# First attention in six slots a batch: row maxima in three fillings of 500 columns, weighted sums in one row

## The chip, the cores and the metric

The kernel runs on one core of a Trainium2 chip. Engines named here: TensorE (PE, with its weight loads PEld), VectorE (DVE), ScalarE (ACT), GpSimd (POOL) and SyncE (SP, which issues most DMAs). The metric is the device time in microseconds of one execution, the median of the runs shown.

## What is computed

Two transformer layers on x of 8 batches x 112 rows x 256 (f32), with a context of 8 x 375 x 256. The part that the change touches is the first of the two attentions, on layer-normalised x, with 16 heads of width 16:

```
q_ = (q @ Wq.T + bq).reshape(B, Sq, HEADS, D_K).transpose(0, 2, 1, 3)
k_ = (k @ Wk.T + bk).reshape(B, Sk, HEADS, D_K).transpose(0, 2, 1, 3)
v_ = (v @ Wv.T + bv).reshape(B, Sk, HEADS, D_K).transpose(0, 2, 1, 3)
scores = jnp.einsum('bhqd,bhkd->bhqk', q_, k_) / jnp.sqrt(jnp.float32(D_K))
attn = jax.nn.softmax(scores, axis=-1)
ctx = jnp.einsum('bhqk,bhkd->bhqd', attn, v_)
...
x = x + _L0_xattn_ref(_layernorm(x), ctx_1024, ctx_1024, ...)
x = x + _L0_ffn_ref(_layernorm(x), ...)      # 8 experts, top 1, 112 rows each
x = x + _L1_xattn_ref(_layernorm(x), ctx_1024, ctx_1024, mask, ...)
x = x + _L1_ffn_ref(_layernorm(x), ...)
```

## The kernel before

**Stages.** After loads and layer norms the first attention runs over the 8 batches (`NB`), and in the same loop each batch's output projection, second layer norm and expert routing follow. Then come the 8 experts, the second attention and the last feed-forward layer. Nothing of the later three stages is edited, except how many blocks of the second attention's value projection (`project_context`, "context projections", 24 in all, each of the shape of a V block) are pulled into gaps of the first.

**The 16 heads** are four groups `g` of four heads `j`; group g = 2m + a. `kt[b % 3]` and `qz` hold K and Q with the heads at rows 32j to 32j + 31, so that four matmuls of one group sit in four row groups of PE and write banks 0 to 3 of PSUM, one each. `qz` holds zeros in the rows of the other parity `a`.

**Three works share banks 0 to 3** in turn:

- `row_max(b, g)` on PE: for a group, 112 x 375 scores per head, only to find the row maxima. DVE reduces them into `mneg` (L1056). Four fillings a batch (MX).
- `scores(b, step)` on PE: the scores transposed (125 keys x 2 x 112 queries, two blocks a step, three steps a batch), to which a matmul of `onesc` with `maxT` adds the negative maxima. ACT takes the exponential into `pT` (L833). Three fillings a batch (ST).
- `weighted(b, step)` on PE reads `pT` and `vones` and adds into bank 4 (PV). It fills none of banks 0 to 3. `pT` has two buffers.

The banks are drained in two halves, LOW (banks 0, 1) and HIGH (2, 3): each has its own semaphores `filled` and `drained`. PE opens a half when the half's last user has drained it (`open_tiles`), and a reader waits for the half's `filled`. So a batch has seven fillings of banks 0 to 3, and each waits for the reader of the one before.

**The slots.** The order is written out by hand. `steps()` runs i from -1 over u in range(SLOTS), and every engine goes through the same list: in slot u of step i PE does `scores(i, SCORE_AT[u])`, `row_max(i + 1, MAX_AT[u])`, `weighted(i, WEIGHTED_AT[u])` and then the stages of `PIPE[u]`, each for batch i minus the number beside it. ACT does in the same slot `exps` and then its share of the stages, DVE `row_max` and then its share. What an engine does is in program order, so a stage's place in `PIPE` is its place in each engine's queue.

**The stages of PIPE.** V0 to V2: V's three blocks. K0, K1: K's two halves. QX, QP: transposes of x and Q for two batches. ND0/ND1 (DVE): the maxima of m = 0, 1 cut into two bf16 pieces (L1069, L1070). NM0/NM1: PE transposes them, ACT copies them to `maxT` (L862). U (ACT, L841): copies bank 4 to `ctxU`. C1: PE transposes `ctxU` after `read(("PV", b))`, that is, after U; DVE divides by the sums (L1075, L1078). C2, C3: transpose and output projection. C4, C5: transpose of the second norm and gate logits. L2, D5, C6, D6: norm and routing. These PE stages use banks 5 to 7 in rotation.

**Loads.** SP asks for the weights of expert e (e = 0 to 3, into `ring`) when scores (e, 0) are filled.

## Time and profile before

| | us |
|---|---|
| median of 3 runs | 377.79 (377.69 to 378.69) |
| the profiled execution | 375.65 |
| its span in the trace | 373.9 |
| PE busy | 354.1 (95%) |
| DVE busy | 182.5 (49%) |
| ACT busy | 149.7 (40%) |
| POOL busy | 57.6 (15%) |

The chain that ended last is PE for 85% of the span. The first attention takes about the first 200 us of it. A PE matmul in f32 appears in the trace as two instructions, so that "x8" is four matmuls. A group's row gives the start of its first instruction, the time to the end of its last, and idle time of the engine just before, in brackets. Groups overlap a little, so the distance between two starts is the time that a group really takes.

### The profile page before, as it was taken

What the parts mean: (1) busy time and instruction counts of PE and PEld (TensorE: products, weight loads), DVE (VectorE), ACT (ScalarE), POOL (GpSimd) and SP (SyncE); (2) the same over time, 40 slices, a digit from 0 to 9 for tenths busy, and PEclk for the clock granted to TensorE, in tenths of its full rate; (3) what the DMA queues carried; (4) which work ended last, traced back from release to release, by engine and by line L of the source; (5) the groups of instructions that cost most, each with busy time, mean ns of one, the idle gap of its engine ahead of it and who ended that gap; (6) DMA issues with size and microseconds to landing.
All of it is one profiled execution on the core that took longest, in us unless ns stands there. A gap on an engine that the chain in (4) does not pass through costs nothing.

```text
span 373.9 us, 7935 instructions
## 1 busy us (share of the span) xinstructions
PE 354.1 (95%) x3108; PEld 266.4 (71%) x3108; DVE 182.5 (49%) x573; ACT 149.7 (40%) x361; POOL 57.6 (15%) x95
## 2 busy tenths in 40 slices
PE   3889999999999999998889999999889999999996
PEld 2446666766657665755668998998768889797875
DVE  4964345647566465564462122212489667532500
ACT  0524553554454553535533221120345667523300
POOL 2730000010101000010120000030694421200000
PEclk9999999999999999999999999999999999999999
DMA  8946060603400100000207499970110011111000
GB/s 245 351 111 227 0 225 3 220 20 96 144 1 15 28 4 13 2 15 2 70 12 213 136 334 335 303 210 25 50 50 1 3 53 52 40 39 50 26 25 25
DMA packets 24885, 35.29 MB, mean 94 GB/s; under 512 B 2608, under 2 KB 21408, under 8 KB 24736
## 3 DMA queue, kind: packets, MB, share of 16 engines
q1 hardware_dynamic: 22160, 31.73, 26.9%
q0 software_dynamic: 768, 1.84, 1.7%
q10 hardware_dynamic: 1920, 1.21, 1.2%
q8 instruction: 25, 0.41, 0.4%
q14 instruction: 12, 0.10, 0.1%
HBM read 31.06 MB, written 3.72 MB: 93 GB/s over the span
## 4 chain that ended last, share of the span: by engine, by line
PE 85%; DVE 6%; DMA 5%; issue 2%; ACT 1%; POOL 0%; SPq 0%; DVEq 0%; ACTq 0%; POOLq 0%
PE ps L417 10%; PE ps L575 8%; PE ps L720 8%; PE ps L585 7%; PE ps L431 7%; PE ps L698 6%; PE ps L454 6%; PE ps L385 6%; PE ps L361 5%; PE ps L651 3%; PE ps L352 3%; DMA xres<-in_x 2%; PE ps L667 2%; PE ps L477 2%; PE ps L521 2%
## 5 line engine op out<-in xcount | busy, mean ns | idle before, releaser
L1056 DVE TENSOR_REDUCE mneg<-ps 112x2 f32<-112x750 f32 x64 | 57.1, 933 | 42.3 <-PE ps L417 41.9
L833 ACT ACTIVATE heads<-ps 125x896 f32<-125x896 f32 x48 | 41.4, 915 | 17.5 <-PE ps L437 17.5
L1273 POOL TENSOR_TENSOR rstd<-veps,neghalf 112x1 f32<-112x1 f32 x32 | 18.5, 577 | 194.1 <-DVE veps L1022 193.9
L417 PE MATMUL ps<-heads 32*112 32x375 f32 x256 | 38.5, 518 | 1.8 <-DVE mneg L1056 1.4
L431 PE MATMUL ps<-heads 32*125 32x224 f32 x384 | 32.2, 374 | 0.7 <-DVE mneg L1056 0.6
L361 PE MATMUL ps<-ctxT,w_in 128*128 128x375 f32 x64 | 25.6, 524 | 7.3 <-DMA ctxT<-in_ctxT 5.9
L575 PEld LDWEIGHTS ps<-xT,ring 128*128 128x128 f32 x256 | 29.8, 192 | 1.1 <-ACT xT L788 0.7
L575 PE MATMUL ps<-xT,ring 128*128 128x112 f32 x256 | 29.9, 275 | 0.4 <-ACT xT L788 0.4
L720 PE MATMUL ps<-heads,ring 128*112 128x256 f32 x128 | 28.8, 382 | 0.0
L585 PE MATMUL ps<-ring,heads 128*112 128x256 f32 x128 | 28.8, 379 | 0.0
L454 PEld LDWEIGHTS ps<-heads,vones 125*17 125x17 f32 x768 | 17.2, 97 | 13.9 <-issue 12.6
L431 PEld LDWEIGHTS ps<-heads 32*125 32x125 f32 x384 | 19.7, 182 | 9.9 <-issue 7.5
L720 PEld LDWEIGHTS ps<-heads,ring 128*112 128x112 f32 x128 | 22.3, 177 | 6.1 <-issue 1.4
L385 PE MATMUL ps<-w_in,ctxT 128*125 128x256 f32 x96 | 25.6, 389 | 0.0
L585 PEld LDWEIGHTS ps<-ring,heads 128*112 128x112 f32 x128 | 22.1, 177 | 4.4
L417 PEld LDWEIGHTS ps<-heads 32*112 32x112 f32 x256 | 14.1, 169 | 15.5 <-issue 9.0
L788 ACT ACTIVATE xT<-ps 128x224 f32<-128x224 f32 x40 | 13.6, 358 | 28.6 <-PE ps L352 28.4
L698 PE MATMUL ps<-xT,heads 128*128 128x224 f32 x128 | 24.9, 353 | 0.0
L454 PE MATMUL ps<-heads,vones 125*17 125x112 f32 x768 | 23.3, 260 | 1.3 <-ACT heads L833 1.3
L698 PEld LDWEIGHTS ps<-xT,heads 128*128 128x128 f32 x128 | 24.0, 190 | 0.1
L477 PE MATMUL ps<-w_in,ctxT 128*125 128x256 f32 x96 | 23.7, 386 | 0.0
L1161 DVE TENSOR_SCALAR heads<-ps,b1col 128x112 f32<-128x112 f32 x32 | 8.5, 326 | 29.8 <-PE ps L575 29.8
(140 smaller groups left out, 523.3 us busy)
## 6 DMA issues: line engine op xcount, KB each, us to landing
ring<-in_L_ffn_W SPq DMA_DIRECT2D x16, 1024.0 KB, 6.7
ctxT<-in_ctxT SPq DMA_DIRECT2D x8, 375.0 KB, 11.0
heads<-in_L_ffn_W SPq DMA_DIRECT2D x2, 1024.0 KB, 10.4
ring<-x_by_odd_rows_dram SPq DMA_DIRECT2D x4, 448.0 KB, 3.6
ring<-in_mask SPq DMA_DIRECT2D x1, 1312.5 KB, 7.4
expert_in_dram<-eo SPq DMA_DIRECT2D x1, 896.0 KB, 11.2
b2row<-in_L_ffn_b SPq DMA_DIRECT2D x8, 112.0 KB, 7.6
out_dram<-ring SPq DMA_DIRECT2D x8, 112.0 KB, 1.9
```

Source lines behind the costliest of these rows:

```text
L361: mm = pe.matmul(o[:, 0:S2], w_in[:, 1, k, m * P:(m + 1) * P], ctxT[:, k, b * S2:(b + 1) * S2], start=k == 0, stop=k == DT - 1)
L385: mm = pe.matmul(o[0:KC, 0:D], ctxT[:, k, b * S2 + c * KC:b * S2 + (c + 1) * KC], w_in[:, 2, k, :], start=k == 0, stop=k == DT - 1)
L417: mm = pe.matmul(bank(j)[0:S, 0:S2], qz[rows, m, a, b * S:(b + 1) * S], kt[b % 3][rows, m, :], start=True, stop=True)
L431: pe.matmul(bank(j)[0:KC, x * QW:(x + 1) * QW].rearrange("p (a q) -> p a q", a=2), kt[b % 3][rows, m, c * KC:(c + 1) * KC], qz[rows, m, :, ...
L454: mm = pe.matmul(bank(4)[32 * j:32 * j + VW, g * S:(g + 1) * S], vones[b % 2][0:KC, c, PAIRS * g + j, :], pT[(SCORE_STEPS * b + step) % 2] ...
L477: mm = pe.matmul(o[0:KC, 0:D], ctxT[:, k, b * S2 + c * KC:b * S2 + (c + 1) * KC], wv_at1[:, k, :], start=k == 0, stop=k == DT - 1)
L575: mm = pe.matmul(o[:, f * S:(f + 1) * S], w1e[e % RING][:, k, ft * P:(ft + 1) * P], xT[:, k, e * S:(e + 1) * S], start=k == 0, stop=k == D ...
L585: mm = pe.matmul(o[0:S, 0:D], hid[e % 2][:, ft, :], w2e[e % RING][:, ft, :], start=ft == 0, stop=ft == FT - 1)
L698: mm = pe.matmul(o[:, f * 2 * S:(f + 1) * 2 * S], w1f[:, k, ft * P:(ft + 1) * P], xT[:, k, 2 * p * S:2 * (p + 1) * S], start=k == 0, stop= ...
L720: pe.matmul(o[0:S, 0:D], gT[p % 2][:, ft, x * S:(x + 1) * S], w2f[:, ft, :], start=ft == 0, stop=False)
L833: act.activation(pT[w % 2][0:KC, pair.start:pair.stop, :], ps[0:KC, pair.start:pair.stop, 0:2 * QW], ACT.Exp, scale=DK ** -0.5).then_inc(f ...
L1056: v.tensor_reduce(mneg[:, b % 2, PAIRS * g + pair.start:PAIRS * g + pair.stop], ps[0:S, pair.start:pair.stop, 0:S2], AX.X, ALU.max, negate ...
```

## The change

- `SLOTS` is 6. The maxima of a batch come in three fillings (`MAX_PARTS`) of 500 columns: group 0 and the first 125 keys of group 1; 250 keys each of groups 1 and 2; group 3 and the last 125 keys of group 2. A filling has two matmuls for each head in place of one. DVE reduces each part apart, those of 125 keys into `mpart`, and joins the two halves of groups 1 and 2 with a minimum (L1099 of the new kernel) ahead of the pieces.
- The three weighted sums of a batch stand in a row in slot 5, so that `pT` needs a third buffer. It lies in the fourth of the experts' ring buffers; expert 3's weights are loaded when batch 6's weighted sums are done. In the last batch the sums stay spread over slots 1, 3 and 5.
- `PIPE` is rearranged. U of batch i - 1 is in slot 0, and C5 is one step later. Q's halves are in two slots (Q0, Q1), and the transposes QX earlier.
- Within scores the matmul with the maxima comes first.
- Context projections: 7 within the slots for 5, 6 ahead of the experts for 7.

```
-SLOTS = 7
+SLOTS = 6
-MAX_AT = {1: 0, 3: 1, 5: 2, 6: 3}
-WEIGHTED_AT = {1: 0, 3: 1, 5: 2}
+MAX_AT = {1: 0, 3: 1, 5: 2}
+MAX_PARTS = (((0, 0, 375), (1, 0, 125)), ((1, 125, 375), (2, 0, 250)), ((3, 0, 375), (2, 250, 375)))
+WEIGHTED_AT = {5: (0, 1, 2)}
+WEIGHTED_LAST = {1: (0,), 3: (1,), 5: (2,)}
 PIPE = {
-    0: [("NM1", 0), ("C1", 1), ("D5", 2), ("V0", -1)],
+    0: [("U", 1), ("NM1", 0), ("C5", 2), ("C1", 1), ("D5", 2), ("V0", -1)],
...
-    6: [("U", 0), ("C5", 1), ("K1", -2), ("ND1", -1)],
+    5: [("ND1", -1)],
 }
-CTX_AT = {(6, 1): 1, (6, 3): 1, (7, 0): 1, (7, 4): 2}
-CTX_BEFORE_EXPERTS = 7
+CTX_AT = {(6, 1): 1, (6, 3): 2, (7, 0): 1, (7, 2): 1, (7, 4): 2}
+CTX_BEFORE_EXPERTS = 6
...
+        pT.append(ring[:, RING - 1, 0:PAIRS * 4 * S].rearrange("p (j n) -> p j n", j=PAIRS))
...
-            def row_max(b, g):
+            def row_max(b, step):
+                for n, (g, lo, hi) in enumerate(MAX_PARTS[step]):
+                    m, a = divmod(g, 2)
+                    at = n * (MAX_PARTS[step][0][2] - MAX_PARTS[step][0][1])
+                    for half, pair in HALVES:
+                        if n == 0:
+                            open_tiles(("MX", b, step), half)
+                        for j in pair:
+                            rows = slice(32 * j, 32 * j + 32)
+                            mm = pe.matmul(bank(j)[0:S, at:at + hi - lo], qz[rows, m, a, b * S:(b + 1) * S],
+                                           kt[b % 3][rows, m, lo:hi], start=True, stop=True)
+                        if n == 1:
+                            mm.then_inc(filled[half], 1)
...
             def exps(b, step):
-                w = SCORE_STEPS * b + step
-                if w >= 2:
-                    act.wait_ge(pv_units, w - 1)
+                if b == NB - 1 and step == 2:
+                    act.wait_ge(pv_units, SCORE_STEPS * b + 1)
+                elif b:
+                    act.wait_ge(pv_units, SCORE_STEPS * (b - 1) + step + 1)
...
+                    if step == 1:
+                        top = mneg[:, b % 2, PAIRS:3 * PAIRS].rearrange("p (g j) -> p j g", j=PAIRS)[:, js, :]
+                        v.tensor_reduce(top, ps[0:S, js, 0:500].rearrange("p j (g k) -> p j g k", g=2), AX.X, ALU.max,
+                                        negate=True).then_inc(free, 1)
+                    else:
+                        top = mneg[:, b % 2, PAIRS * MAX_PARTS[step][0][0]:][:, js]
+                        v.tensor_reduce(mpart[:, step // 2, js], ps[0:S, js, 375:500], AX.X, ALU.max, negate=True)
+                        v.tensor_reduce(top, ps[0:S, js, 0:375], AX.X, ALU.max, negate=True).then_inc(free, 1)
...
-            for e in range(RING):
+            for e in range(RING - 1):
                 wait_filled(("ST", e, 0, HIGH))
                 load_expert(e)
...
+            sp.wait_ge(pv_units, SCORE_STEPS * (NB - 1))
+            load_expert(RING - 1)
```

ACT around the copy to `ctxU`, before, from the last exponential of one batch to the first two of the next (`heads<-ps 125x896` are exponentials of the two halves, `vones` is V's copy, `xT` C4's, `ex` C5's, `heads<-ps,bcol` K's):

```order
L862 ACTIVATE maxT<-ps 128x224 [waits high_tiles_filled,bank7_filled]
L841 ACTIVATE ctxU<-ps 128x448 [waits bank6_filled,pv_units_done]
L868 ACTIVATE ex,small<-lg,small 112x8 [waits logit_max_ready]
L797 ACTIVATE heads<-ps,bcol 128x375 [waits bank6_filled,high_tiles_filled]
L833 ACTIVATE heads<-ps 125x896 [waits low_tiles_filled,pv_units_done]
L833 ACTIVATE heads<-ps 125x896 [waits high_tiles_filled]
L862 ACTIVATE maxT<-ps 128x224 [waits high_tiles_filled,bank7_filled]
L817 ACTIVATE vones<-ps 125x16x16 [waits bank6_filled,pv_units_done]
```
And in the changed kernel:

```order
L888 ACTIVATE maxT<-ps 128x224 [waits high_tiles_filled,bank5_filled]
L859 ACTIVATE heads<-ps 125x896 [waits low_tiles_filled,pv_units_done]
L859 ACTIVATE heads<-ps 125x896 [waits high_tiles_filled]
L867 ACTIVATE ctxU<-ps 128x448 [waits bank5_filled,pv_units_done]
L888 ACTIVATE maxT<-ps 128x224 [waits high_tiles_filled,bank6_filled]
L894 ACTIVATE ex,small<-lg,small 112x8 [waits logit_max_ready]
L842 ACTIVATE vones<-ps 125x16x16 [waits bank6_filled,pv_units_done]
```
The copy to `ctxU` stood ahead of the two exponentials of the next batch's first scores; now it stands behind both.

PE, before, the last weighted sums of a batch, then C4, NM0, the fourth maxima filling and C5:

```order
L454 MATMUL ps<-heads,vones 17x112 [waits high_tiles_drained,low_tiles_drained]
L454 MATMUL ps<-heads,vones 17x112 x15
L352 MATMUL ps<-ident,xn 128x112 [waits bank7_drained,normalised_ready]
L352 MATMUL ps<-ident,xn 128x112
L499 MATMUL ps<-identb,mpieces 128x112 [waits bank5_drained,max_pieces_ready]
L499 MATMUL ps<-identb,mpieces 128x112
L417 MATMUL ps<-heads 112x375 [waits low_tiles_drained,bank7_drained,bank6_drained]
L417 MATMUL ps<-heads 112x375
L417 MATMUL ps<-heads 112x375 [waits high_tiles_drained]
L417 MATMUL ps<-heads 112x375
L531 MATMUL ps<-wg,xT 112x8 [waits bank6_drained,bank7_drained]
L531 MATMUL ps<-wg,xT 112x8
```
The same queue from the end of the next batch's first scores on (NM1, the transposes of C1, V's block, the first maxima filling):

```order
L499 MATMUL ps<-identb,mpieces 128x112 [waits bank5_drained,max_pieces_ready]
L499 MATMUL ps<-identb,mpieces 128x112
L507 MATMUL ps<-ident,ctxU 112x128 [waits bank6_drained,bank4_drained]
L507 MATMUL ps<-ident,ctxU 112x128 x3
L385 MATMUL ps<-w_in,ctxT 125x256 [waits bank7_drained]
L385 MATMUL ps<-w_in,ctxT 125x256
L417 MATMUL ps<-heads 112x375 [waits low_tiles_drained,bank6_drained,bank5_drained]
L417 MATMUL ps<-heads 112x375
L417 MATMUL ps<-heads 112x375 [waits high_tiles_drained]
```
In the changed kernel PE has the three weighted sums of a batch in a row, in slot 5:

```order
L479 MATMUL ps<-heads,vones 17x112 [waits bank6_drained,low_tiles_drained,high_tiles_drained,bank7_drained,bank4_drained]
L479 MATMUL ps<-heads,vones 17x112 x15
L479 MATMUL ps<-heads,vones 17x112 [waits high_tiles_drained,low_tiles_drained]
L479 MATMUL ps<-heads,vones 17x112 x15
L479 MATMUL ps<-ring,vones 17x112 [waits high_tiles_drained,low_tiles_drained]
L479 MATMUL ps<-ring,vones 17x112 x15
```
The next batch's first scores follow directly, and from their end on PE has:

```order
L524 MATMUL ps<-identb,mpieces 128x112
L556 MATMUL ps<-wg,xT 112x8 [waits bank7_drained]
L556 MATMUL ps<-wg,xT 112x8
L532 MATMUL ps<-ident,ctxU 112x128 [waits bank5_drained,bank4_drained]
L532 MATMUL ps<-ident,ctxU 112x128 x3
L405 MATMUL ps<-w_in,ctxT 125x256 [waits bank6_drained]
L405 MATMUL ps<-w_in,ctxT 125x256
L441 MATMUL ps<-heads 112x375 [waits bank5_drained,bank6_drained,low_tiles_drained]
L441 MATMUL ps<-heads 112x375
L441 MATMUL ps<-heads 112x375 [waits high_tiles_drained]
L441 MATMUL ps<-heads 112x375
L441 MATMUL ps<-heads 112x125 x4
```
The transposes reading `ctxU` (L507 before, L532 now) wait for bank 4 in both, with V's block and the next maxima filling behind them; the gate logits (`ps<-wg,xT`) now stand just ahead of them, and the filling behind has 375 and 125 columns.

## Rows read from the trace of the kernel before

**Rows 1.** Six batches: us, busy time (instructions) by engine, PE clock, DMA share, GB/s.

```profile
47.88:171.78 123.90, 122.80 (x1476) 80.13 (x1474) 71.79 (x208) 60.77 (x126) 8.44 (x11) 1.00 0.18 59
```
**Rows 2.** Order of time, PE, batch 2: start, us, engine, line, what, count, [idle before].

```profile
67.62 0.27 PE L499 MATMUL ps<-identb,mpieces 112*128 112x112 bf16 x2
67.73 0.61 PE L507 MATMUL ps<-ident,ctxU 128*112 128x128 f32 x4
68.18 1.03 PE L385 MATMUL ps<-w_in,ctxT 128*125 128x256 f32 x4
69.13 1.25 PE L417 MATMUL ps<-heads 32*112 32x375 f32 x8
70.31 0.97 PE L454 MATMUL ps<-heads,vones 125*17 125x112 f32 x32
71.21 0.41 PE L514 MATMUL ps<-ident,cc 112*128 112x112 f32 x2
...
73.19 1.12 PE L521 MATMUL ps<-w_in,ccT 128*112 128x256 f32 x4
...
75.01 0.55 PE L352 MATMUL ps<-ident,xn 112*128 112x112 f32 x4
75.49 0.90 PE L417 MATMUL ps<-heads 32*112 32x375 f32 x8
76.32 0.97 PE L454 MATMUL ps<-heads,vones 125*17 125x112 f32 x32
```
**Rows 3.** Order of time, PE, the second half of the same batch.

```profile
78.58 1.68 PE L377 MATMUL ps<-xT,w_in 128*128 128x224 f32 x8
80.19 0.66 PE L431 MATMUL ps<-heads 32*125 32x224 f32 x8
...
81.37 1.13 PE L385 MATMUL ps<-w_in,ctxT 128*125 128x256 f32 x4
82.58 1.60 PE L417 MATMUL ps<-heads 32*112 32x375 f32 x8
...
86.29 0.56 PE L531 MATMUL ps<-wg,xT 128*112 128x8 f32 x4
86.70 1.51 PE L361 MATMUL ps<-ctxT,w_in 128*128 128x375 f32 x4
```
**Rows 4.** Order of time, ACT, the first exponentials of batch 2.

```profile
67.72 1.73 ACT L833 ACTIVATE heads<-ps 125x896 f32<-125x896 f32 x2
69.33 0.36 ACT L862 ACTIVATE maxT<-ps 128x224 bf16<-128x224 bf16 x1
```
**Rows 5.** The line that copies bank 4: durations in ns, min/median/max.

```profile
L841 ACT ACTIVATE ctxU<-ps x8: 537/550/550, 44.3 to 183.9; 128x448 f32<-128x448 f32 x8
```
**Rows 6.** Order of time, DVE, batch 2.

```profile
66.32 0.16 DVE L1096 TENSOR_REDUCE small<-ps 112x1 f32<-112x8 f32 x1
...
68.45 0.26 DVE L1075 RECIPROCAL rden<-ps 112x16 f32<-112x16 f32 x1 [1.26 <-PE ps L507]
...
70.19 1.78 DVE L1056 TENSOR_REDUCE mneg<-ps 112x2 f32<-112x750 f32 x2
```
**Rows 7.** Order of time, PE: what follows the first scores of batches 0 and 1.

```profile
27.26 0.27 PE L499 MATMUL ps<-identb,mpieces 112*128 112x112 bf16 x2
...
47.88 0.27 PE L499 MATMUL ps<-identb,mpieces 112*128 112x112 bf16 x2
```
**Rows 8.** Order of time, PE, batch 7: after its first scores; its last weighted sums.

```profile
171.78 0.27 PE L499 MATMUL ps<-identb,mpieces 112*128 112x112 bf16 x2
...
173.75 0.97 PE L454 MATMUL ps<-heads,vones 125*17 125x112 f32 x32 [0.39 <-ACT heads L833]
...
183.25 0.41 PE L352 MATMUL ps<-ident,xn 112*128 112x112 f32 x2
...
184.54 0.65 PE L507 MATMUL ps<-ident,ctxU 128*112 128x128 f32 x4
```
**Rows 9.** The page's DMA issues: the experts' weights, KB each, us to landing.

```profile
ring<-in_L_ffn_W SPq DMA_DIRECT2D x16, 1024.0 KB, 6.7
```

93 lines of the change are left out of this document (45 added, 48 removed).

## The prediction

> **What bounds the kernel now.** I read first the busy time over the stretch from the end of batch 1's first scores to the end of batch 7's (six whole batches): TensorE (PE) is busy 122.80 of 123.90 us at a granted clock of 1.00 [rows 1], so 20.65 us a batch go by with hardly an idle gap. That reads as "bound by PE", but a matmul's record covers waits within a group of them. So I read the order of time next, start to start. A filling of banks 0 to 3 takes 0.83 us when nothing holds it (75.49 to 76.32 [rows 2]) and 1.54 us when the exponentials are not out of the upper half yet (82.58 to 84.12 [rows 3]). Scores take 1.18 us free (80.19 to 81.37 [rows 3]). What is under the cover of busy PE is a second chain: PE fills banks 0 to 3, ACT or DVE empties them, PE fills again. Seven such turns make a batch. The links, from end to end of the PE groups:
>
> - scores to the end of the next maxima filling: 67.62 to 70.31 = 2.69 us [rows 2]. In it the two exponentials run from 67.72 to 69.45 [rows 4], and 0.86 us of filling follow.
> - maxima to the end of the next scores: 70.31 to 73.19 = 2.88 us [rows 2]. The two reductions end at 70.19 + 1.78 = 71.97 [rows 6], and scores end 1.22 us later.
>
> Where PE has much to do between two fillings, PE's work is the longer (81.37 minus 76.32 = 5.05 us with weighted sums, K and Q [rows 2, 3]). So the kernel stands with both limits close to each other, and the question of the change is the next limit at each of the six turns.
>
> **The change, turn by turn.** *Maxima.* The columns are the same 1500 a batch, in three fillings of 500. A free filling is 0.83 us for 375 columns in two passes; 125 more columns add between 0 (hidden) and a further third of it, 0.28. I take 0.21, the streaming part alone: 1.04 us, and 0.86 + 0.21 = 1.07 after a late release. One turn goes away, and with it one reduction pair. On DVE a reduction of 2x375 = 750 elements recurs after 0.85 us (1.78 for two, about 0.93 for one) and one of 8 elements takes 0.16 [rows 6]: about 1.04 ns an element beyond 0.16. The middle filling reduces 1000 per half: 1.20 us, pair about 2.30. The outer ones reduce 250 and 750 per half: 0.33 + 0.85 twice plus the last end, about 2.44. All six together 7.2 us a batch against 4 x 1.78 = 7.1. The two small minima add about 0.2 us each, ahead of the casts, where PE stands at least 1.2 us of scores behind; they cost nothing on the path.
>
> A halves' effect is lost: before, the lower half's `filled` was signalled as soon as its own matmuls were in; now the second part of the lower half comes behind the upper half's first, so both halves report at the end and DVE begins about 0.1 us after it. So maxima to scores is 0.1 + 2.44 + 1.22 = 3.76 us (outer) and 3.62 (middle); scores to maxima is 2.69 + 0.21 = 2.90.
>
> *Chain alone.* 3 x 2.90 + 2 x 3.76 + 3.62 = 19.84 us a batch, against 20.65 measured now: 0.8 us less.
>
> *PE's work in each turn.* Behind maxima 0: C2, K (1.4 us: 86.70, four of 1.51 [rows 3]), C6, in even batches one half of Q (1.61 / 2 = 0.8; 78.58 to 80.19 [rows 3]) and scores: 3.8 us even, 3.0 odd, against 3.76. Behind scores 1: C3 and V, 73.19 to 75.01 = 1.82 [rows 2], and 1.04: 2.86 against 2.90. Behind maxima 1: K, Q and scores 3.4 against 3.62. Behind scores 2: V, C4, NM0 1.3 and 1.04: 2.4 against 2.90. Behind maxima 2: three weighted sums. Now each is 0.90 (70.31 to 71.21 [rows 2]); the 32 instructions are about 0.023 apart, so 96 take 2.4 rather than 2.7; with scores 3.6 against 3.76. All of this fits under the chain to 0.1 us; I take 0.05 a batch.
>
> *The moved copy.* This decides. `U` copies the sums out of bank 4 for the transposes of C1. Before, ACT did it in slot 6, ahead of the next exponentials, and C1 started with no wait, 0.11 us after scores (67.73 [rows 2]). Now ACT has it in slot 0 behind both exponentials of that slot, while PE has C1 in the same slot, ahead of V and of the next maxima filling. ACT's engine takes its instructions in order: exponentials start 0.10 after the scores' end, the next copy starts 1.61 us after that (67.72 to 69.33 [rows 4]), `ctxU` takes 0.55 [rows 5]. So C1 starts 0.10 + 1.61 + 0.55 + 0.05 = 2.31 us after the scores' end. Only NM1 (0.11) and C5 (86.29 to 86.70 = 0.41 [rows 3]) lie in that gap: 1.8 us of PE idle. Then C1 0.45 and V 0.95 [rows 2] and the filling 1.04 follow: scores to maxima 0 is 4.75 us and not 2.90, +1.85. Queued behind C1 are V, the maxima filling, and through it DVE's reductions and the next scores; DVE's C1 work, 1.74 us from 68.45 to the reduction at 70.19 [rows 6], just ends as the filling does. The batch is 19.84 + 1.85 + 0.05 = 21.74 us against 20.65: **+1.1 us, six times: +6.6.**
>
> The Trainium skill (PSUM — Partial Sum Buffer, "Engine vs sequencer instructions") states that ScalarE's queue is strict FIFO and that matmuls keep program order. By that rule neither engine gets around the wait; the trace agrees in that the exponentials and the copy behind them stand one after another.
>
> *Batch 0* has no C1 before it: ends of its scores and of batch 1's are 27.26 and 47.88 [rows 7], 20.62 us; the chain gives 19.84: -0.8. *Ahead of it* the fillings and reductions of batch 0 stand in line: three pairs of about 2.4 us for four of 1.78, each with less head start, and a cast before NM0 with less cover. Between -0.5 and +1.0; I take +0.4.
>
> *Batch 7.* No maxima. Scores end at 171.78 and the first weighted sums start at 173.75, 1.97 us later [rows 8]. Now C1 (2.31 + 0.45) and one context projection (0.95, the shape of a V) lie ahead of them: 3.71, so +1.75. The projection added in slot 2 falls into time in which PE waited for exponentials: 0. At the end `U` no longer waits behind the copy for C4: C1 started at 184.54, 1.3 us after the weighted sums ended [rows 8]; now 0.7: -0.6. From there to the experts the same chain runs (C2, C3, normalise, C4, C5, scatter), and the seventh projection before the experts was filling for it, so its removal gains nothing there; bound -0.9 to 0. Expert 3's weights are asked for at the end of batch 6 instead of in batch 3. A megabyte lands in 6.7 us [rows 9], and batch 7 and three experts lie ahead of their use: 0.
>
> *The reversed order within scores* has the same instructions. Its last one is now the f32 pass; bounds 0 to +0.1 us a filling, at most +2 in all; I take 0.
>
> **Sum.** 6.6 - 0.8 + 0.4 + 1.75 - 0.6 = +7.4 us. The profiled execution took 375.65 us (span 373.9) and would take 383.0; the median of the runs is 377.79, and **377.8 + 7.4 = 385.2 us**, 2.0% more.
>
> **Rivals.**
>
> *The wait costs nothing.* If bank 4 were copied before the exponentials, or C1 stood where PE needs it late, the same sum without 6 x 1.85, and with 1.75 gone, gives 7.4 - 11.1 - 1.75 = -5.4: 372.4 us. The order of both engines speaks against it; for it speaks only that the exponentials hold the next filling for 1.83 us anyway, so that the wait is partly paid already (which the sum has in it). C1 costs nothing if it starts within 2.90 - 1.04 - 0.95 - 0.45 = 0.46 us of the scores' end; the point from which the whole is faster than now is 1.2 us (7.4 of the 12.85 us must go). 12%.
>
> *Switching and filling are dearer than I think, and their saving larger.* Between groups of differently shaped matmuls some 0.15 us pass (0.90 a group against 32 x 0.023 = 0.74 [rows 2]). Seven groups of this kind a batch become four; if PE's work and not the chain were the limit in most turns, 0.45 a batch go, 3.2 in all: 382.0 us, range 379 to 382.5. Against it: five of six turns are the chain's. 9%. The Trainium skill (TensorEngine Tiling (Array Packing), "Key Properties") says that changing the tiling mode drains the engine, which is this rival's mechanism; by it the change gains, by the sum above only under waits.
>
> *The chain is longer still.* The second part of each filling costs 0.29 rather than 0.21 (four weight loads in a row), the last f32 pass delays ACT by 0.1, the reductions of 250 cost a full start each: 0.24 + 0.3 + 0.2 = 0.7 a batch, +5: 390.2. 15%.
>
> *The gains and the wait cancel* within 0.3%, the copy starting some 1 us sooner than I have it: 4%.
>
> **How the numbers follow.** The first sum has 60%, with a range of its own of 382.5 to 388. With the rivals the 80% range is 380.5 to 390. About 0.3% is what a measurement of this kernel tells from no change: faster 0.12, same 0.04, slower 0.84.
>
> **What would show it.** In the new profile the copy `ctxU` stands right behind the second exponential, and the transposes reading `ctxU` show an idle of about 1.8 us before them, seven times, 11 to 14 us in total, with ACT `ctxU` as releaser. The distance between first scores is 21.5 to 22 us in even and odd batches alike (before, 21.8 and 20.0). DVE's reductions pair to 2.4 us. Without that idle the forecast is wrong, and the time should be below 377; with it and a batch of 21 us or less, my links of the chain are too long.

## The result, and the profile after

The changed kernel takes **393.52 us** (median of 4 runs, 393.28 to 395.25) against 377.74 us (377.29 to 378.69, 4 runs) for the kernel before in the same comparison: ratio 1.041, 95% interval 1.038 to 1.044. The forecast was 385.2 us with 380.5 to 390 as its range. The sign is right; the size is more than twice the one predicted, and the time lies outside the range. Ratios, here and below, leave out executions more than 1.5% above the fastest of their kernel, while medians and ranges take in all of them.

The page of the changed kernel (span; busy time by engine; TensorE's granted clock in 40 slices, in tenths; the maxima, the copy and the weighted sums among the costly groups):

```profile
span 391.7 us, 8243 instructions
PE 355.8 (91%) x3236; PEld 277.1 (71%) x3236; DVE 187.2 (48%) x605; ACT 150.0 (38%) x361; POOL 57.4 (15%) x95
PEclk9998989989899999999898999999999999999999
...
L441 PE MATMUL ps<-heads 32*112 32x375 f32 (+2 forms) x384 | 34.9, 429 | 0.1
...
L1089 DVE TENSOR_REDUCE mpart<-ps 112x2 f32<-112x250 f32 x32 | 13.2, 413 | 38.6 <-PE ps L441 38.6
...
L1090 DVE TENSOR_REDUCE mneg<-ps 112x2 f32<-112x750 f32 x32 | 29.7, 929 | 0.0
```

Its waits (who waited for whom: us in total, times, longest). The wait that the forecast put first is there, eight times and 12.5 us, seven of them at the starts of batches 1 to 7 (2.07 us in batch 1, which has no C5 to fill it, and 1.71 or 1.72 in the others):

```profile
PE ps L532 <- ACT ctxU L867: 12.5, 8, 2.1
```

**The wait, in the order of time.** The start of batch 4, PE (start, us, engine, line, what, count, [idle before]):

```profile
120.02 0.27 PE L524 MATMUL ps<-identb,mpieces 112*128 112x112 bf16 x2
120.13 0.52 PE L556 MATMUL ps<-wg,xT 128*112 128x8 f32 x4
122.36 0.65 PE L532 MATMUL ps<-ident,ctxU 128*112 128x128 f32 x4 [1.72 <-ACT ctxU L867]
122.85 1.03 PE L405 MATMUL ps<-w_in,ctxT 128*125 128x256 f32 x4
123.81 1.11 PE L441 MATMUL ps<-heads 32*112 32x375 f32 x16
124.85 0.41 PE L539 MATMUL ps<-ident,cc 112*128 112x112 f32 x2
```

and of batch 2, PE and then ACT, whose rows show why PE waits:

```profile
74.00 0.27 PE L524 MATMUL ps<-identb,mpieces 112*128 112x112 bf16 x2
...
76.34 0.65 PE L532 MATMUL ps<-ident,ctxU 128*112 128x128 f32 x4 [1.71 <-ACT ctxU L867]
76.83 1.71 PE L405 MATMUL ps<-w_in,ctxT 128*125 128x256 f32 x4
78.47 2.02 PE L441 MATMUL ps<-heads 32*112 32x375 f32 x16
80.42 0.41 PE L539 MATMUL ps<-ident,cc 112*128 112x112 f32 x2
```

```profile
74.13 1.73 ACT L859 ACTIVATE heads<-ps 125x896 f32<-125x896 f32 x2 [4.05 <-PE ps L461]
75.74 0.55 ACT L867 ACTIVATE ctxU<-ps 128x448 f32<-128x448 f32 x1
```

Up to the transposes (L532) both batches are alike: 2.34 us from the scores' end to C1, 1.7 of it idle. Behind them they are not. V (L405) takes 1.03 us in one and 1.71 in the other, the maxima filling (L441) 1.04 (to 124.85) and 1.95 (to 80.42). Windows say what it is, four of the second stretch, then one behind the wait of batch 3 and one behind that of batch 4 (us, busy time and instructions of PE, PEld, DVE, ACT, POOL; granted clock; DMA share; GB/s):

```profile
74.00:76.30 2.30, 0.63 (x10) 0.53 (x6) 0.53 (x4) 2.17 (x4) 0.00 (x0) 1.00 0.42 59
76.30:77.50 1.20, 1.16 (x7) 1.03 (x8) 0.44 (x2) 0.51 (x3) 0.00 (x0) 0.80 1.05 433
77.50:78.50 1.00, 1.00 (x7) 0.34 (x5) 0.90 (x6) 0.00 (x0) 0.00 (x0) 0.50 0.99 402
78.50:80.40 1.90, 1.90 (x17) 1.08 (x16) 0.21 (x2) 0.38 (x1) 0.00 (x0) 0.50 1.07 378
...
100.50:102.50 2.00, 2.00 (x12) 1.01 (x14) 1.37 (x8) 0.38 (x1) 0.00 (x0) 0.60 0.00 0
123.20:125.20 2.00, 2.00 (x23) 1.26 (x22) 1.56 (x9) 0.38 (x1) 0.00 (x0) 1.00 0.00 0
```

PE was busy 0.63 of 2.30 us, and 0.7 us after it took up work again its granted clock went to 0.50 (the lower level, 1.2 GHz): 0.80 over 76.30 to 77.50 puts the fall near 77.0, and it lasts until about 80.4. In batch 4, after the same wait, it stayed at 1.00. DMA traffic is not the difference: batch 3's fall comes with no DMA at all (share 0.00).

**Where the time went.** The table goes by the starts of the transposes of the maxima behind a batch's first scores (L524; L499 before), as in [rows 7]; such a start is called the batch's mark. The kernel before has two traces; the second one, of the experiments below, took 377.78 us, as the median does, and is the partner here.

| stretch | before, 2 traces | after | difference to the 2nd | predicted |
|---|---|---|---|---|
| start to the first maxima filling | 14.71, 15.28 | 17.39 | +2.1 | 0 |
| from there to batch 0's mark | 12.55, 12.45 | 13.30 | +0.85 | +0.4 |
| batch 0 | 20.62, 20.61 | 20.04 | -0.6 | -0.8 |
| batches 1 to 6 | 123.90, 123.89 | 135.78 | +11.9 | +6.6 |
| batch 7's mark to the first expert | 29.10, 30.80 | 32.10 | +1.3 | +1.15 |
| the rest | 173.0, 173.0 | 173.1 | +0.1 | 0 |
| span | 373.9, 376.0 | 391.7 | +15.7 | +7.4 |

The six batches last 23.27, 23.30, 22.72, 21.72, 23.06 and 21.71 us after, in place of 19.74, 21.78, 20.02, 21.77, 20.02, 20.57. The two in which the clock held (4 and 6) stand at the predicted 21.74. So 6 x (21.72 - 20.65) = 6.4 us is the wait as costed, and the 5.5 us on top, in four batches, is the clock.

Three rows are less sure than they look. The end fits its forecast by luck: a second trace of the changed kernel (the last experiment) has 30.57 us there, so that the difference is anything from -0.2 to +3.0 us with the four traces, and two of the four have half clock in it. The same second trace has 13.70 us from the first filling to batch 0's mark, +1.25 and not +0.85, and 175.7 us in the rest, +2.7, with 10 us of half clock in it.

### The profile page after: what moved, and what is told of

Read it like the earlier page. It is cut to its first block, busy times and chain, and to the rows that moved or that the text cites. A ratio compares the mean times of both kernels' runs of the same rounds, so it can differ in the third digit from the quotient of the medians.

```text
span 391.7 us, 8243 instructions
## 1 busy us (share of the span) xinstructions
PE 355.8 (91%) x3236; PEld 277.1 (71%) x3236; DVE 187.2 (48%) x605; ACT 150.0 (38%) x361; POOL 57.4 (15%) x95
## 4 chain that ended last, share of the span: by engine, by line
PE 80%; DVE 9%; ACT 4%; issue 3%; DMA 3%; POOL 0%; SPq 0%; ACTq 0%; DVEq 0%; POOLq 0%
PE ps L441 8%; PE ps L600 7%; PE ps L745 7%; PE ps L610 7%; PE ps L723 6%; PE ps L405 6%; PE ps L479 5%; PE ps L461 5%; PE ps L502 4%; PE ps L381 4%; DVE mneg L1085 3%; PE ps L676 3%; DVE mneg L1090 3%; PE ps L456 3%; PE ps L546 2%
## 5 line engine op out<-in xcount | busy, mean ns | idle before, releaser
L859 ACT ACTIVATE heads<-ps 125x896 f32<-125x896 f32 x34 | 29.3, 915 | 43.0 <-PE ps L461 43.0
L441 PE MATMUL ps<-heads 32*112 32x375 f32 (+2 forms) x384 | 34.9, 429 | 0.1
L1089 DVE TENSOR_REDUCE mpart<-ps 112x2 f32<-112x250 f32 x32 | 13.2, 413 | 38.6 <-PE ps L441 38.6
L441 PEld LDWEIGHTS ps<-heads 32*112 32x112 f32 x384 | 20.2, 188 | 15.0 <-issue 6.0
L1090 DVE TENSOR_REDUCE mneg<-ps 112x2 f32<-112x750 f32 x32 | 29.7, 929 | 0.0
L405 PE MATMUL ps<-w_in,ctxT 128*125 128x256 f32 x96 | 28.2, 421 | 0.0
L461 PE MATMUL ps<-heads 32*125 32x224 f32 x384 | 28.1, 366 | 0.0
L1350 POOL DMA_INDIRECT expert_in_dram<-xn,idx_put x8 | 8.0, 1000 | 128.3 <-DVE idx_put L1155 128.3
L502 PE MATMUL ps<-w_in,ctxT 128*125 128x256 f32 x96 | 25.9, 411 | 0.0
L456 PE MATMUL ps<-maxT,onesc 2*125 2x224 bf16 x192 | 19.1, 282 | 5.9 <-DVE mneg L1090 4.1
L381 PEld LDWEIGHTS ps<-ctxT,w_in 128*128 128x128 f32 x64 | 12.4, 216 | 15.9 <-issue 12.4
```

The source lines that it names most:

```text
L381: mm = pe.matmul(o[:, 0:S2], w_in[:, 1, k, m * P:(m + 1) * P], ctxT[:, k, b * S2:(b + 1) * S2], start=k == 0, stop=k == DT - 1)
L405: mm = pe.matmul(o[0:KC, 0:D], ctxT[:, k, b * S2 + c * KC:b * S2 + (c + 1) * KC], w_in[:, 2, k, :], start=k == 0, stop=k == DT - 1)
L441: mm = pe.matmul(bank(j)[0:S, at:at + hi - lo], qz[rows, m, a, b * S:(b + 1) * S], kt[b % 3][rows, m, lo:hi], start=True, stop=True)
L456: pe.matmul(bank(j)[0:KC, x * QW:(x + 1) * QW], onesc[rows, :], maxT[rows, m, :], start=True, stop=False)
L461: mm = pe.matmul(bank(j)[0:KC, x * QW:(x + 1) * QW].rearrange("p (a q) -> p a q", a=2), kt[b % 3][rows, m, c * KC:(c + 1) * KC], qz[rows, ...
L502: mm = pe.matmul(o[0:KC, 0:D], ctxT[:, k, b * S2 + c * KC:b * S2 + (c + 1) * KC], wv_at1[:, k, :], start=k == 0, stop=k == DT - 1)
```

## The experiments

A label below names a run; batches are listed 0 to 6. The theory after this reading: (1) the copy behind the exponentials costs 1.85 us a batch; (2) the same wait makes the clock fall in most batches; (3) without the wait the new arrangement is the faster one. The rival: the loss sits in the arrangement (dearer fillings, the row of 96 weighted sums, the other order within scores), and the wait only shows it.

### The copy ahead of the exponentials

In ACT's loop the copy to `ctxU` is issued at the head of slot 0, and no longer among the stages behind the exponentials:

```diff
             for i, u in steps():
+                if u == 0 and 0 <= i - 1 < NB:
+                    post("U", i - 1)
...
                 for stage, b in extras(i, u):
+                    if stage == "U":
+                        continue
```

> The changed kernel with one edit: ACT copies bank 4 to ctxU ahead of the two exponentials of slot 0 and not behind them. Theory A (the wait of C1 is the whole loss, partly by itself and partly because PE's clock falls to half after it): the idle of 1.7 to 2.1 us before the transposes of ctxU goes, the granted clock stays at 1.00 in the first attention, batches last about 19.9 us instead of 21.7 to 23.3, and the median is 371 to 375 us, below the kernel before. Rival B (the three fillings of 500 columns and their longer reductions are a good part of the loss): batches stay at 21 us or more and the median is 380 us or more. Rival C (the clock falls for another reason): the idle goes, but stretches at half clock stay, median 376 to 382 us.

382.75 us, ratio to the kernel before 1.0085 [1.0053, 1.0117]; batches 20.24, 19.58, 21.14, 21.14, 21.14, 21.42, 21.14. Of the 15.8 us lost, most are back, but it is no gain, and the 371 to 375 us of the expectation are missed. Batch 1 shows the chain without this wait, 19.58 (I had 19.84). From batch 2 on a second wait stands where the first one was (waits, then PE in batch 3):

```profile
PE ps L405 <- ACT maxT L888: 5.2, 5, 1.0
```

```profile
91.18 0.27 PE L524 MATMUL ps<-identb,mpieces 112*128 112x112 bf16 x2
91.29 0.52 PE L556 MATMUL ps<-wg,xT 128*112 128x8 f32 x4
91.66 0.63 PE L532 MATMUL ps<-ident,ctxU 128*112 128x128 f32 x4
93.34 1.13 PE L405 MATMUL ps<-w_in,ctxT 128*125 128x256 f32 x4 [1.05 <-ACT maxT L888]
```

NM1, C5, C1 and V0 take the spare banks 5 to 7 in turn, so V0 gets NM1's bank; and the copy that empties it (`maxT`) stands on ACT behind the two exponentials, as the first copy did. C5 in slot 0, moved there by the change, is what makes V0 the third filling after NM1. Batch 1 has no C5, and no such wait. The granted clock stayed at 1.00 behind all six waits of 1.05 us (batches 2 to 7).

### V ahead of C1

```diff
-    0: [("U", 1), ("NM1", 0), ("C5", 2), ("C1", 1), ("D5", 2), ("V0", -1)],
+    0: [("U", 1), ("NM1", 0), ("C5", 2), ("V0", -1), ("C1", 1), ("D5", 2)],
```

> The changed kernel with one edit: in slot 0 the V block stands ahead of C1, on PE, so that part of the same wait is covered by work (ACT's order is as in the changed kernel). Theory A: PE's idle before C1 is about 0.8 us instead of 1.7, too short for the clock to fall; scores to maxima take 2.31 + 0.45 + 1.04 = 3.8 us, a batch 20.8 us, median 378 to 381. If the clock falls after 0.8 us of idle as well: 383 to 386. Rival B: about 390.

387.48 us, 1.0255 [1.0188, 1.0322], more than either value expected (378 to 381, or 383 to 386 with the clock falling); batches 20.05, 20.77, 21.80, 21.79, 21.80, 22.07, 21.79. Batch 1 is as it should be, the others lose a microsecond to the same bank, now at C1:

```profile
93.79 1.11 PE L405 MATMUL ps<-w_in,ctxT 128*125 128x256 f32 x4
95.99 0.62 PE L532 MATMUL ps<-ident,ctxU 128*112 128x128 f32 x4 [1.09 <-ACT maxT L888]
96.54 1.11 PE L441 MATMUL ps<-heads 32*112 32x375 f32 x16
```

PE's wait is 1.1 us here, and the granted clock is 1.00 over the six batches. In batch 7, where a wait of 1.72 us for `ctxU` is left, it falls (182.9 to 186.3 us). From batch 2 on a batch is as long as one of the changed kernel in which the clock held, 21.8 against 21.7, and yet the ratio is 1.6% lower (1.0255 for 1.0413). In the traces batches 1 to 6 are 5.8 us shorter, of which batch 1, with less wait, is about 1 (20.77 for 21.72 at full clock): the rest is the clock's share.

### The kernel before, with its copy late

```diff
-    0: [("NM1", 0), ("C1", 1), ("D5", 2), ("V0", -1)],
+    0: [("U", 1), ("NM1", 0), ("C1", 1), ("D5", 2), ("V0", -1)],
...
-    6: [("U", 0), ("C5", 1), ("K1", -2), ("ND1", -1)],
+    6: [("C5", 1), ("K1", -2), ("ND1", -1)],
```

> The kernel before with one edit: U moved from the end of slot 6 to the head of slot 0, so ACT copies bank 4 behind the two exponentials, as in the changed kernel; everything else (seven slots, four fillings of 375, spread sums) as before. Theory A: PE idles some 2.1 us before C1 in seven batches, and the wait moves the first maxima filling by about 2.1 us against a turn that was 2.69: 1.85 to 2.2 us a batch directly, 13 us, and 3 to 8 more where the clock falls: median 391 to 399 us. Rival B: under 385 us.

403.86 us, 1.0642 [1.0594, 1.069]: the one moved copy costs the kernel before 6.4%, more than the whole change cost, and more than I expected. Batches 20.62, 21.99, 25.59, 22.27, 25.59, 22.26, 24.08. The idle is 2.04 us at each start. Half clock follows it in batches 2, 4, 6 and 7 and not in 1, 3 and 5. Where the clock held, a batch is 2.25 us longer than in the kernel before (21.99 for 19.74, 22.27 for 20.02, 22.26 for 20.02): that is the wait by itself. Where it fell, it is 3.5 to 3.8 us longer. Batch 2:

```profile
75.28 0.99 PE L507 MATMUL ps<-ident,ctxU 128*112 128x128 f32 x4 [2.04 <-ACT ctxU L841]
76.07 1.91 PE L385 MATMUL ps<-w_in,ctxT 128*125 128x256 f32 x4
77.91 1.34 PE L417 MATMUL ps<-heads 32*112 32x375 f32 x8
```

The first two groups took 0.61 and 1.03 us in [rows 2]. So neither wait nor clock needs the fillings of 500 columns, nor anything else of the new arrangement.

### Narrow matmuls in the wait

C5's two matmuls (8 columns each) are made six times over, so that 12 of them, 24 instructions in the trace, stand in the wait; the result is the same.

```diff
-                    for k in range(DT):
-                        mm = pe.matmul(o[0:S, 0:E], xT[:, k, b * S:(b + 1) * S], wg[:, k, :],
-                                       start=k == 0, stop=k == DT - 1)
+                    for _ in range(6 if b < NB - 1 else 1):
+                        for k in range(DT):
+                            mm = pe.matmul(o[0:S, 0:E], xT[:, k, b * S:(b + 1) * S], wg[:, k, :],
+                                           start=k == 0, stop=k == DT - 1)
```

> The changed kernel with the wait left in and PE kept busy in it: the gate logits' matmuls (C5) are issued six times instead of once (same sums, five of the six left out of nothing; only repeated). Batches with C5 are 2 to 7, so five or six of the seven waits are covered. Theory A, clock part: with PE active the granted clock stays at 1.00 behind the wait, those batches last 21.7 to 21.9 us instead of up to 23.3, and the median is 386 to 389 us against 393.5. If the clock has nothing to do with the idle: 393 to 395 us.

397.84 us, 1.0497 [1.0426, 1.0569]: not faster, rather slower. Batches 21.07, 22.71, 21.79, 23.06, 21.80, 23.71, 23.36. They fill the wait, and the clock falls behind it all the same in batches 3, 5, 6 and 7 (and in batch 1, which has no C5). The windows of batch 3:

```profile
94.75:97.00 2.25, 2.25 (x28) 2.25 (x25) 0.00 (x0) 2.12 (x4) 0.00 (x0) 1.00 0.00 0
97.00:99.00 2.00, 2.00 (x16) 1.29 (x15) 1.42 (x9) 0.68 (x4) 0.00 (x0) 0.80 0.00 0
99.00:101.00 2.00, 2.00 (x18) 1.16 (x18) 0.55 (x4) 0.38 (x1) 0.00 (x0) 0.50 0.04 8
```

PE's record is full (2.25 of 2.25 us), and 0.80 over 97 to 99 us puts the fall near 98.2, a microsecond after the transposes at 97.2. Batches 2 and 4 (21.79, 21.80) held. The expectation failed: this filling did not keep the clock. So the theory can't be put as "idle PE, falling clock"; what was left to test was whether PE did too little in the wait.

### Wide matmuls in the wait

The changed kernel with four matmuls of 128 x 125 x 256 ahead of C5, in C5's bank and overwritten by it, in batches 2 to 7.

```diff
                     o = open_bank(("LG", b), n)
+                    if b < NB - 2:
+                        for k in range(4):
+                            pe.matmul(o[0:KC, 0:D], ctxT[:, k % 2, b * S2:b * S2 + KC], w_in[:, 2, k % 2, :],
+                                      start=k == 0, stop=k == 3)
```

> The changed kernel with its waits left in and wide work added in the first of them: ahead of the gate logits, in the same bank and overwritten by them, four f32 matmuls of 128 x 125 x 256 (some 1.8 us; results unused), in steps 2 to 7. busy_in_the_wait, with 20 extra matmuls of 8 columns, kept the clock in four batches (21.8 us) and lost it in three (22.7 to 23.7). If the clock falls because PE does too little in the stretch: no half clock in batches 2 to 7, each 21.7 to 21.9 us, median 386 to 389 us. If it falls for a reason that has nothing to do with the wait: 393 us or more.

391.31 us, 1.0295 [1.0249, 1.0341]. By the ratios that is 1.2% below the changed kernel, with more work in it: about 4.5 us. In microseconds it misses what I expected (386 to 389), since in this comparison the kernel before also stood 2.2 us higher; in the trace it is as expected. Batches 20.02, 23.27, 21.71, 21.71, 21.72, 21.99, 21.71: the clock falls in batch 1, which has no C5 and so no cover, and the covered ones stand at the forecast's 21.74. Batch 2:

```profile
73.85 0.27 PE L524 MATMUL ps<-identb,mpieces 112*128 112x112 bf16 x2
73.95 1.95 PE L557 MATMUL ps<-w_in,ctxT 128*125 128x256 f32 x8
75.74 0.47 PE L560 MATMUL ps<-wg,xT 128*112 128x8 f32 x4
76.19 0.65 PE L532 MATMUL ps<-ident,ctxU 128*112 128x128 f32 x4
76.67 1.03 PE L405 MATMUL ps<-w_in,ctxT 128*125 128x256 f32 x4
77.63 1.11 PE L441 MATMUL ps<-heads 32*112 32x375 f32 x16
```

This is the test of the clock by itself: C1 starts 2.34 us behind the mark as before, the arrangement is the same, PE is at work in the wait, and V and the filling are back to 0.96 and 1.04 us. The granted clock is 1.00 behind the waits of batches 2 to 7, six of six. (The "20 extra matmuls" of the expectation are instructions, 10 matmuls; and of the six batches with them the clock held in two.)

### Both waits taken away

The copy first, and C5 back in slot 5, one step earlier:

```diff
-    0: [("U", 1), ("NM1", 0), ("C5", 2), ("C1", 1), ("D5", 2), ("V0", -1)],
+    0: [("U", 1), ("NM1", 0), ("C1", 1), ("D5", 2), ("V0", -1)],
...
-    5: [("ND1", -1)],
+    5: [("C5", 1), ("ND1", -1)],
```

> u_first with a second edit: C5 (gate logits) is back at the end of the slots, in slot 5 one step earlier, as in the kernel before, so that V's block in slot 0 no longer takes the PSUM bank of NM1, which ACT frees only behind the two exponentials. u_first showed batch 1, which has no C5, at 19.58 us and all later ones at 21.14, with V waiting 1.05 us for the copy to maxT. Theory A2 (the loss is two waits for ACT in slot 0, the copy to ctxU and the copy to maxT, and the six-slot form by itself is a gain): batches 19.6 to 20.0 us, some 1.3 us less than u_first in six of them, median 371 to 376 us, below the kernel before. Rival B2 (the form itself costs): 379 us or more.

379.88 us, 0.9983 [0.9948, 1.0017]; batches 21.23, 20.13, 20.30, 20.25, 20.31, 20.53, 20.25. Of both waits one instance is left (1.5 us, in batch 7), and from 50 to 195 us the clock is 1.00, but the batches are 0.3 above the upper end of what I expected. C5's 0.41 us stands in the turn of the weighted sums, ahead of scores, which has nothing over.

On this kernel two parts were undone by themselves. The weighted sums spread over slots 1, 3 and 5 again:

```diff
-WEIGHTED_AT = {5: (0, 1, 2)}
+WEIGHTED_AT = {1: (0,), 3: (1,), 5: (2,)}
```

> The kernel u_first_c5_back with the three weighted sums of a batch put back into slots 1, 3 and 5 (WEIGHTED_AT as in the kernel before; pT keeps three buffers). It prices the row of sums alone. The chain of banks 0 to 3 sets the batch, and spread sums lie in the turns behind the maxima, where K and Q already fill the time: turn 0 grows by up to 0.9 us, turn 1 by 0.9 less what it now waits, the last shrinks to the chain's 3.7. Expected: batches 20.4 to 21.2, median 377 to 383 us, 4 to 8 above u_first_c5_back. If the row gives only its saved switches (0.45 us a batch): 3 us above.

383.15 us, 1.0107 [1.0067, 1.0147]. By the ratios that is 1.24% or 4.7 us more than with the row, inside the 4 to 8 expected; the medians differ by 3.3 us only, which is nearer to the 3 us that the saved switches alone would give. The batches tell the two apart: 21.41, 20.03, 21.32, 21.54, 21.87, 20.00, 20.93. Batches 1 and 5 are no longer than with the row (20.13, 20.53), though they have the same three separate groups, so the switches are worth nothing that shows. Batches 2 and 4, at a granted clock of 1.00, are 1.0 and 1.6 us longer. There the sums lie in turns that Q already fills. Batch 4, then the same turn with the row:

```profile
116.28 1.36 PE L441 MATMUL ps<-heads 32*112 32x375 f32 x16
117.56 0.97 PE L479 MATMUL ps<-heads,vones 125*17 125x112 f32 x32
...
121.00 0.32 PE L456 MATMUL ps<-maxT,onesc 2*125 2x224 bf16 x4
```

```profile
114.06 1.27 PE L441 MATMUL ps<-heads 32*112 32x375 f32 x16
...
117.81 0.32 PE L456 MATMUL ps<-maxT,onesc 2*125 2x224 bf16 x4
```

From filling to scores go 4.72 us and not 3.75. The turn of slot 5 is now short of work, and PE idles 0.77 us in it in each of the seven batches, the two short ones too. Behind two of the seven the clock falls, at 93.7 us (0.67 in 93 to 95 us, 0.50 in 95 to 97) and at 175.6:

```profile
91.96 0.31 PE L456 MATMUL ps<-maxT,onesc 2*125 2x224 bf16 x2 [0.77 <-DVE mneg L1094]
...
93.87 1.91 PE L405 MATMUL ps<-w_in,ctxT 128*125 128x256 f32 x4
```

So the row of 96 is worth having here: it takes the sums out of two full turns and fills one that is short of work. The 0.3 us of streaming is not what it saves.

And the old order within scores, f32 pass first (the two `pe.matmul` calls of L456 and L461 exchanged, `start` and `stop` with them):

> The kernel u_first_c5_back with the order within scores put back (f32 matmul first, maxima added last). In the prediction this was taken at 0 with bounds of 0 to +0.1 us a filling for the new order. Expected: within 1 us of u_first_c5_back; if ending on the f32 matmul costs 0.1 us in 21 fillings, 2 us below it; if the bf16 matmuls ahead save time because they run while the upper half is awaited, 1 to 3 us above it.

383.35 us, ratio 1.0008 [0.9966, 1.0049]; batches 21.36, 20.16, 20.35, 20.31, 20.36, 20.59, 20.30, 0.05 us above the other. In the batches, and by the ratios, which overlap, the order is worth nothing that can be measured, as the forecast had it. The median is 3.5 us higher than without this edit. The profiled execution, 385.45 us, has 13.7 us of half clock far behind the batches (274.1 to 287.8 us), and nothing here shows that the order has a part in it.

### C5 where the turn has room, and a second trace of the kernel before

```diff
-    0: [("U", 1), ("NM1", 0), ("C5", 2), ("C1", 1), ("D5", 2), ("V0", -1)],
-    1: [("C2", 1), ("K0", -2), ("C6", 2), ("D6", 2)],
+    0: [("U", 1), ("NM1", 0), ("C1", 1), ("V0", -1)],
+    1: [("C2", 1), ("K0", -2)],
...
-    4: [("V2", -1), ("C4", 1), ("NM0", -1)],
-    5: [("ND1", -1)],
+    4: [("C5", 2), ("D5", 2), ("V2", -1), ("C4", 1), ("NM0", -1)],
+    5: [("ND1", -1), ("C6", 2), ("D6", 2)],
```

> The changed kernel with the copies of ctxU ahead of the two wide exponentials of slot 0 (as in u_first) and C5 and D5 posted in slot 4, C6 and D6 in slot 5, of the same step. Theory (each batch's length is the chain of scores and maxima, wherever no other wait stands on it): with ctxU copied early PE doesn't stand behind the exponentials, with C5 out of slot 0 V0 finds its bank free, and C5's 0.41 us now lies in a turn between a maxima-add and the next scores where DVE's two instructions (2.3 to 2.4 us) leave PE some 0.5 us over. Batches of 19.8 to 20.0 us against 20.3 in u_first_c5_back, no stretch of half clock behind the batches' starts, span 374 to 376, and 376.5 to 378.5 us in time, ratio 0.992 to 0.996. Rival one: C5's place doesn't matter and the 20.3 of u_first_c5_back has another cause: batches stay at 20.3 and the ratio at 0.998. Rival two: moved there, C5 comes before ctxU of the same step is copied in and PE waits again: batches above 20.5, ratio above 1.0.

Batches 19.97, 19.58, 19.72, 19.77, 19.76, 19.77, 19.77: as expected or a little shorter, and 0.9 us below the 20.65 of the kernel before in each of six. The clock is 1.00 throughout (71.10 to 169.89 us). The time is 378.64 us, 0.9973 [0.9941, 1.0004], just outside both ranges expected and no gain clear of noise; the gain of the batches is 6.2 us and most of it does not arrive. Against the second trace of the kernel before, the profiled execution loses it in four places. The first maxima filling stands at 18.02 us, not 15.28. From there to batch 0's mark go 13.53 us, not 12.45. From batch 7's mark to the first expert go 31.24 us, not 30.80, and the rest takes 174.1, not 173.0, with half clock from 265.2 to 272.0 us. In the third place PE has two waits that the kernel before doesn't have, for the gate and routing stages that were moved, with half clock behind the second (0.53 over 193.4 to 197.0 us):

```profile
189.56 0.38 PE L372 MATMUL ps<-ident,xn 112*128 112x112 f32 x2 [0.85 <-DVE lg L1138]
...
193.17 0.21 PE L566 MATMUL ps<-onehot,tri 112*112 112x8 bf16 x1 [0.90 <-DVE onehot L1143]
```

All its executions show such a loss of clock: their mean granted clock is 0.968 to 0.982, that of the kernel before in the same comparison 0.990 to 0.995. At 0.982 that is some 13 us of half clock in an execution, at 0.995 some 4 (an estimate, twice the missing share of the span). So the clock outside the batches takes back a part of what the batches gain.

The kernel before once more, unchanged, for the start:

> The kernel before, unchanged, for a second trace of it. Theory: the 2.7 us by which the first middle maximum stood later in the changed kernel's profile (17.39 against 14.71 us) are the start-up's own variation, since the instructions up to it are the same: it should stand between 15 and 18 us here too, the span should be 374 to 378 us, and the batches should be those of the first trace (20.62, 19.74, 21.78, 20.02, 21.77, 20.02, 20.57) within 0.1 us. If the first trace is typical instead, the maximum stands at 14.7 again and the change must have moved it.

377.78 us, span 376.0; batches within 0.01 us of the first trace. The first filling stands at 15.28 us, so the head of the first trace was ordinary. The ends of the two differ: from batch 7's mark to the first expert 30.80 us against 29.10, with the clock at 0.81 in 194 to 203 us. The kernel before has such falls too, only few.

### The same, with the head's wait filled

```diff
-        if first <= i - behind < NB:
+        if first <= i - behind < NB and (stage, i) != ("V0", 0):
             yield stage, i - behind
+    if (i, u) == (-1, 5):
+        yield "V0", 1
```

> u_first_c5_d5_in_slot_4 with one projection moved in the start alone: the first V projection of batch 1 (two blocks, 1.03 us at full clock) stands in the slot before the first scores instead of behind the first transposes of the maxima. Theory: in u_first_c5_d5_in_slot_4 PE stands 1.50 + 0.77 us in wait of VectorE ahead of the first scores and runs the 5 us behind it at half clock or near; the projection fills about 1 us of that wait, and is missing from the turn behind, which VectorE's 2.4 us leave short of work by less. The first scores' stretch gets 0 to 0.3 us later, the turn behind it 1.0 to 2.5 us shorter (the more, the fewer matmuls run at half clock), all batches after it stay at 19.7 to 19.8. Span 373 to 375 us, ratio to the kernel before 0.989 to 0.995. Rival: the fall of the clock comes all the same and the place behind is bound by VectorE, not PE: within 0.5 us of u_first_c5_d5_in_slot_4, ratio 0.996 to 0.999.

Ratio **0.990 [0.986, 0.994]** to the kernel before, the only arrangement here whose interval lies below 1, with a caveat that follows. From the first filling to batch 0's mark 12.62 us (13.53 without the edit), batch 0 19.25 (19.97), the others unchanged. PE (start, us, what, idle before):

```profile
27.38 1.13 PE L407 MATMUL ps<-w_in,ctxT 128*125 128x256 f32 x4
28.95 0.31 PE L458 MATMUL ps<-maxT,onesc 2*125 2x224 bf16 x2 [0.45 <-DVE mneg L1096]
```

The caveat: the ratio rests on the better six of its 12 executions (372.1 to 380.0 us in all); over all of them the medians are 377.18 and 377.99, a ratio of 0.998, so the gain is there in its better executions and nearly vanishes in the rest. Its times follow the clock. The two executions with a mean granted clock of 0.995 took 372.12 and 372.55 us, the eight with 0.977 took 376.50 to 379.99; the kernel before, at 0.990 to 1.000, took 375.72 to 379.77. The profiled execution took 379.99 us. It has half clock from 191.1 to 197.9 us, around the second of the two waits for the moved gate and routing stages, and from 269.6 to 279.8 us, far behind everything that was edited. Whether the first of the two can be had back by placing these stages otherwise was not tried.

### The changed kernel once more

> The changed kernel once more, for the start: the first K and Q matmuls behind PE's first wait (1.35 us in both kernels) ran at half clock in its first trace and at full clock in both traces of the kernel before. Theory: that is the start-up's own variation, the first middle maximum may stand at 15.1 to 18.1 us, and the seven batches again at 21.7 (where the clock holds) or 22.7 to 23.3 (where it falls), the falls not necessarily at the same batches as in the first trace. Rival: the clock's falls are tied to places of this kernel, and the same batches (1, 2, 3, 5) fall again.

394.77 us, span 393.0. The first filling at 15.10 us: so the 2 us at the start of the first trace are not the change's. Batches 19.98, 23.00, 23.35, 23.06, 21.71, 23.62, 23.19: batches 1, 2, 3 and 5 fall again, 4 holds again, and 6 falls where it held before. The rival was half right: mostly the same places, not all. In 7 starts with this wait (batch 7 included, where it fell in the first trace and held this time) the clock fell five times in each trace. The six batches last 137.9 us, 7.6 more than six of 21.72.

## Why the prediction was right and wrong

**Right: the wait, its place and its own price.** C1 was to start 2.31 us after the scores (2.34), PE to idle 1.8 (1.7), a free filling to take 1.04 (1.04), a batch 21.74 (21.71 and 21.72 wherever the clock held). ACT's copies do stand behind its exponentials; `u_first` shows that the order alone makes that wait. The Trainium skill's rule of strict FIFO (PSUM — Partial Sum Buffer, "Engine vs sequencer instructions") was the right one to lean on; the traces agree, for `ctxU` (1.71 us of idle) and for the second copy, `maxT` (1.05), too.

**Right: the chain and the parts at nothing.** DVE's pairs: 0.42 + 0.93 + 0.41 + 0.93, from 80.59 to 83.03 = 2.44 us, as summed. The chain alone came to 19.84 us a batch; free of waits it runs at 19.6 to 19.8. The reversed order costs nothing in the batches (0.05 us), and in the first trace what follows the first expert's start is 0.1 us longer, so the later loading of expert 3's weights costs nothing either.

**Wrong: the term "6 x +1.1".** It gave +6.6 us and measured +11.9. It took every duration behind the wait from rows at a granted clock of 1.00 [rows 1, 2] and never asked what 1.7 us without work do to that clock. The clock fell to half for 3 to 4 us in most batches, which cost 5.5 us in the profiled execution, 7.6 in the second trace, on top of the 6.4 of the wait. `wide_work_in_the_wait` shows the link: with PE given real work in the same wait the clock held in six of six, and the batches were the predicted 21.7 us. None of the rivals had it; the one at 390.2 us was the nearest in size, by other reasons. Rows that could have warned me were few: at clock 1.00 in all six batches, [rows 1] says only what happens without waits. The Trainium skill (TensorE: Matmul & The Clock Gate, "A second HAM failure mode: psum-queue depth-cycling") describes short idles of PE between groups as a cause of a clock that goes down and up. The traces agree (0.50 behind eight of twelve idles of 1.7 us and both of 2.07), and that page was the one to weigh against this change.

**Wrong by omission: the second wait.** "If the copy were earlier" was costed at 372.4 us. It measured 382.75, because under the first wait lay another, on NM1's bank: 1.05 us of idle and 1.56 us a batch (21.14 for 19.58). The forecast read the moves of C5 as filling for the gap and didn't follow its bank. With both gone and C5 moved it is still 379.88 and 378.64: the batches gain 0.4 and 0.9 us each, and what lies before and behind them takes most of that back, part of it at a lower clock. So the third part of the theory, that the new arrangement is the faster one without the wait, holds for the batches and is not shown for the whole.

**Start and end.** Ahead of batch 0: +0.75 to +0.85 for +0.4 by the first trace, inside the bound of +1.0, and +1.15 to +1.25 by the second, outside it. There PE waits 1.50 + 0.77 us for DVE in the changed kernel, and some of the matmuls behind run at half speed (granted clock 0.50 from 29.2 to 32.7 us in the first trace). Batch 7: weighted sums started 4.35 us after the scores' mark in one trace (half clock in the projection) and 3.78 in the other, for a predicted 3.71. The very start (14.7 to 18.5 us to the first filling) is variation between executions: the four K matmuls behind PE's first wait take 1.50 us in four of the fourteen traces and 2.84 in ten. That this too is the clock can't be read from the windows, which give 1.00 there in both cases. But the traces also hold each change of the granted clock with its time. The first entry, of 1.00, begins at 9.5 to 10.0 us in the four, and in the ten at 14.4 to 17.4 us, when these matmuls are over. With the ratio of 1.9 between the two times, that makes it the clock; no entry gives its value ahead of that.

**The sum by its terms, measured:** wait 6.4 (6.6), clock 5.5 (0), batch 0 -0.6 (-0.8), ahead of it 0.85 (0.4), batch 7 and the end 1.3 (1.15), the start 2.1 (0), rest 0.1: 15.7 us against 7.4. The terms of the end and of the start hang on which traces are paired (above); the clock's is 7.6 by the second trace; the wait's is the same. The chance of "slower", 0.84, was well placed. The range was too narrow since all its bounds came from rows at full clock.

**Open:** what decides whether a given wait of 1.7 us makes the clock fall. Same rows ahead, same wait, and two outcomes; nor does the fall stand at a fixed distance from the wait: it came between 0.5 us before and 1.3 us after PE took up work again. Narrow matmuls in the wait left it undecided (it held in two of six), wide ones held it in six of six.
